# Second cross-attention: the expert-output gathers issued at the first row maximum of a tile instead of behind the row statistics

## The reference, cut to what matters

```python
# x: rows after the second attention; y: expert outputs; gw: the two gate weights of a row
x  = x + gw[:, 0] * y[first expert of the row] + gw[:, 1] * y[second expert of the row]
h  = layernorm(x)                      # rows of the queries, second cross-attention
q  = h @ Wq + bq ;  k = ctx @ Wk + bk ;  v = ctx @ Wv + bv      # 16 heads of 16
p  = softmax(q k^T / 4 + mask)         # 64 queries x 256 keys per sequence and head
x  = x + (p v) @ Wo + bo
```

## Time and profile before

| what | value |
|---|---|
| runs of the kernel before | 1083.7, 1084.77 and 1091.38 us, median 1084.77 us |
| the profiled execution | 1086.17 us, span of its instructions 1084.4 us |
| busy share of the span | TensorE 94%, VectorE 59%, ScalarE 44%, GpSimd 22% |
| second cross-attention | from about 736 to 900 us of the span |
| gathers of this stage | 16, in 8 pairs, 0.94 to 1.04 us each on GpSimd |

### The profile page before, as it was taken

The page is one execution under the profiler, slowest core; times in us unless marked ns, Lnnn a source line. Parts: engine busy times, 40 slices in busy tenths (PEclk is TensorE's granted clock), DMA queues, the critical chain, the costliest instruction groups (busy, mean ns, idle before and its releaser), DMA issues.

```text
span 1084.4 us, 27524 instructions
## 1 busy us (share of the span) xinstructions
PE 1021.5 (94%) x11715; PEld 880.5 (81%) x11715; DVE 639.6 (59%) x1376; ACT 472.6 (44%) x866; POOL 243.7 (22%) x381
## 2 busy tenths in 40 slices
PE   5999999999999899999489999997999998999998
PEld 5888888888887787887389999996888876887887
DVE  5655555455234355775749999976566653454342
ACT  3333333333333656543146677753434333364231
POOL 2311311211211033342403444323211100011000
PEclk9999999999999899998589999999999999999999
DMA  9400000000000800220136567713111002000000
GB/s 298 138 2 21 21 1 21 2 1 1 1 1 10 332 2 3 80 99 12 50 79 233 195 198 273 238 42 88 41 47 35 3 2 68 5 2 2 1 21 19
DMA packets 55672, 72.79 MB, mean 67 GB/s; under 512 B 8504, under 2 KB 48896, under 8 KB 54912
## 3 DMA queue, kind: packets, MB, share of 16 engines
q1 hardware_dynamic: 54016, 66.85, 18.4%
q0 software_dynamic: 1536, 4.20, 1.3%
HBM read 60.02 MB, written 11.01 MB: 66 GB/s over the span
## 4 chain that ended last, share of the span: by engine, by line
PE 83%; DVE 7%; ACT 4%; issue 3%; another core or an unknown queue 1%; POOL 1%; DMA 1%; DVEq 0%; POOLq 0%; ACTq 0%
PE ps L615 8%; PE ps L630 8%; PE ps L2178 7%; PE ps L2194 6%; PE ps L2534 5%; PE ps L1476 4%; PE ps L599 3%; PE ps L647 3%; PE ps L1124 3%; PE ps L1394 3%; PE ps L667 3%; PE ps L1433 2%; PE ps L1493 2%; PE ps L569 2%; PE ps L1049 2%
## 5 line engine op out<-in xcount | busy, mean ns | idle before, releaser
L371 POOL TENSOR_TENSOR rn_tmp<-rn_cur,eps 128x1 f32<-128x1 f32 x48 | 14.6, 304 | 427.1 <-DVE rn_cur L365 427.0
L750 ACT ACTIVATE x0pT<-ps 128x512 f32<-128x512 f32 x64 | 38.4, 600 | 123.5 <-PE ps L630 123.5
L2330 DVE CAST eh_hi<-eh 128x512 fp32r<-128x512 f32 x60 | 69.9, 1165 | 13.7 <-ACT eh L2240 13.7
L2178 PE MATMUL ps<-moe_xT_hi,ew_1hi 128*128 128x256 f32 x240 | 69.7, 290 | 2.3 <-DVE moe_xT_lo L2324 2.3
L2194 PE MATMUL ps<-ew_2hi,eh_hi 128*128 128x256 f32 x240 | 69.4, 289 | 2.4 <-DVE eh_lo L2332 2.4
L2178 PE MATMUL ps<-moe_xT_lo,ew_1hi 128*128 128x256 f32 x240 | 68.8, 287 | 0.0
L2178 PE MATMUL ps<-moe_xT_hi,ew_1lo 128*128 128x256 f32 x240 | 68.7, 286 | 0.0
L2194 PE MATMUL ps<-ew_2hi,eh_lo 128*128 128x256 f32 x240 | 67.0, 279 | 0.0
L2194 PE MATMUL ps<-ew_2lo,eh_hi 128*128 128x256 f32 x240 | 66.9, 279 | 0.0
L2534 PE MATMUL ps<-f,ffw 128*128 128x512 f32 x256 | 60.4, 396 | 0.2 <-DVE f L2507 0.2
L859 DVE TENSOR_TENSOR x0A_lo<-ps,x0A_hi 128x512 fp32r<-128x512 f32 x64 | 41.1, 685 | 31.8 <-ACT x0A_hi L741 31.7
(11 more groups left out here) (330 smaller groups left out, 2827.1 us busy)
## 6 DMA issues: line engine op xcount, KB each, us to landing
ew<-L_ffn_W_dram SPq DMA_DIRECT2D x30, 1024.0 KB, 7.0
x0cin<-ctx_dram SPq DMA_DIRECT2D x8, 512.0 KB, 4.3
x1cin<-ctx_dram SPq DMA_DIRECT2D x8, 512.0 KB, 4.6
xg<-moe_in SPq DMA_DIRECT2D x15, 256.0 KB, 7.6
moe_out<-moe_y SPq DMA_DIRECT2D x15, 256.0 KB, 7.6
moe_in<-padneg SPq DMA_DIRECT2D x3, 1024.0 KB, 12.9
maskrow<-mask_BxS_ik_dram SPq DMA_DIRECT2D x2, 1024.0 KB, 7.5
x0wk<-L_xattn_Wkv_dram SPq DMA_DIRECT2D x1, 1024.0 KB, 9.1
```

The costliest lines, as they stand in the source:

```text
L750: nc.scalar.activation(g.pT[:, u, :], ps[:, S_BANK[u % 2], :], ACT.Exp, scale=64.0 ** -0.5).then_inc(C0.exp, 1)
L2178: last = nc.tensor.matmul(ps[:, n % 3, j * BT:j * BT + BT], w[b % 2][:, i, f * P:f * P + P], v[b % 2][:, i, :], start=(i == 0 and m == 0), ...
L2330: nc.vector.tensor_copy(eh_hi[n % 3][:, :], eh[n % 3][:, :]).then_inc(MO.hi, 1)
```

## The change

GpSimd's order in the second cross-attention is written as a loop over the iterations. The pair of gathers of tile t+2 is now issued in iteration t, behind a wait for `C1.s_ps` at 2t+1, the signal that also starts VectorE's first maximum of tile t. The sets of statistics keep their order, and no other engine's program changes.

```diff
         def pool_x1(pool):
             for t in range(2):
                 moe_collect(pool, t)
-            for phase, t in X1_ROWS:
+            def rstd(phase, t):
                 row_rstd(pool, t, X1_ROWS[phase, t] % 2, phase, X1_ROWS[phase, t])
-                if phase == "x1" and t + 2 < T:
+
+            rstd("x1", 0)
+            rstd("x1", 1)
+            for t in range(T):
+                if t + 2 < T:
+
+                    pool.wait_ge(C1.s_ps, 2 * t + 1)
                     moe_collect(pool, t + 2)
+                if t > 0:
+                    rstd("attn", t - 1)
+                if t + 2 < T:
+                    rstd("x1", t + 2)
+            rstd("attn", T - 1)
```

## The result

The changed kernel takes **1097.34 us** in the median of 17 runs, the kernel before 1084.96 us in 17 runs beside it: ratio **1.0092** [1.0070, 1.0115], 0.9% slower. The forecast was 1080.6 us, and 1097.34 lies outside its range. The ratio leaves out three runs of the changed kernel that count as slow (1102.1 to 1102.6 us; the median of the other 14 is 1095.1), and the profiled execution, which took 1102.3 us, is one of the three.

The account below looks back on a forecast made before the run. TensorE was taken to bound the kernel (83% of the time). Terms -3.93 (tiles 5 to 7), -0.52 (tile 4) and +0.25 (iteration 0) sum to -4.2 us, from the median 1084.77 to 1080.6 us; range 1078 to 1087 us.

Parts of the forecast that it names:

- the 1.31 us: Second cross-attention, iterations 1 to 3: each 1.31 us longer because late gathers hold back TensorE's completion signal to ScalarE.
- the 4.45 of the sum: Gain from removing six pairs from their old places: 3.93 us for tiles 5 to 7, 0.52 for tile 4.
- The recorder's case: Rival: late signals exist only in the profiled execution, or are not the gathers' doing; no effect, 1084.8 us; chance 0.27.
- cost 0: Pairs under the first maximum: a transposes' signal held 0.4 us is covered by VectorE's 0.51 us idle, so 0.
- The half case: Rival: TensorE's own stream is held in `fill_pv`, 0.52 us in five pairs; 1083.2 us; chance 0.11.
- -3.93: Iterations 1 to 3: moving the pairs of tiles 5, 6 and 7 away saves 3 x 1.31 = 3.93 us.
- tile 4's 0.52: Iteration 0: tile 4's pair stretches the last exponent group on TensorE from 0.45 to 0.97 us; removing it saves 0.52.
- Iteration 0: New pair just behind the scores: late transposes' signals delay the next steps by at most 0.5 us; taken as 0.25.
- The data's lateness: Gathered data arrive later before their use in the combine, but still in time: cost 0.
- VectorE's cost: First maximum beside a pair still takes 2.29 us like all others: cost 0.
- GpSimd's wait: GpSimd's added wait for the scores' signal: only roots of statistics over 6 us later stand behind it, cost 0.
- The moved hold: Rival: transposes' signals held 2.14 us at the new place, delaying the second maximum; +2.1 us, 1086.8 us; chance 0.12.

Follow-up runs that it names:

- eight buffers: Kernel before with eight `yg` buffers instead of four, tiles 2 to 7 gathered two at a time behind the first three roots: 1078.62 us on A, 1083.27 us on C.
- the doubled kernel: Changed kernel with each pair of gathers issued twice, the first time into buffers that nobody reads: 1118.76 us on B, ratio 1.0328.

## Why the prediction was wrong

**Where the 1.31 us are, and whose they are: right.** All three recordings of the kernel before have the long beats, and in iterations 1 to 3 alone. Without the late gathers, with plain transfers, or with the pairs elsewhere they are gone, and on B and C the clock-free time falls by 3.7 to 4.7 us, near the 4.45 of the sum (by 0.9 only with eight buffers, which lose in iteration 0 what the loop saves). The plain transfers with the memsets show that it is the indirect transfers.

**The recorder's case: wrong.** Recorded and unrecorded runs agree at equal clock, and on B and C the timed runs of versions without held signals in the loop are faster in clock-free time. The Trainium skill, page "SBUF — State Buffer", section "SBUF: two separate sides", has it that TensorE and ScalarE never wait on anyone; here TensorE was stopped for 0.40 and 0.42 us beside a pair and ran through beside memsets. I did not show whether the memory's ports are what it stands for.

**The step that failed: "cost 0" for the new place.** I looked at which signals fall into the window and found the thin transposes. But a pair beside the dense small matmuls also stops TensorE's own stream: 1.37 us per pair in five iterations, 6.85 us, where I took 0 and named 0.52 as the upper bound. I had taken that bound from the one place where I had seen the stream stretch, the very end of a pair, and had not asked what a whole pair costs under a dense stream. The trace of the kernel before had a row that warned, and I overlooked it, though it stands beside the earlier trace rows: the scatters there start at 499.01 and 500.36, and the 64 matmuls of 18 columns that begin at 500.63 are broken for 0.43 us (the row at 501.81 above) and take 2.79 us, where the 64 that begin at 518.39, 2.0 us behind the start of the next pair, take 2.04 and are not stopped. That is 0.75 us with only the later part of a pair beside the stream; for a whole pair no row bounded the price from above, and the range should have said so. The half case was this mechanism, at less than half its size. With the right size the sum is -3.93 - 0.39 (iteration 0: 17.00 for 17.39, tile 4's 0.52 less 0.13) + 6.85 = +2.5 us.

**The term that was missing: the clock.** +2.5 us would have given 1087.3, slower than before and 0.3 above the upper end of the range. The rest is the granted clock, of which the prediction does not speak. Two falls of 6.83 us followed stopped streams in the first recording, one in the second, five in the doubled kernel, and none between 760 and 899 us in the eleven recordings of kernels that have no pair under `fill_pv` (seven of them not from A). By the mean clocks longer falls came more often too: on B 6 of 11 timed runs of the changed kernel had a mean clock of 0.960 to 0.965, which a fall of 6.83 us alone doesn't give, and the lowest of the 28 runs of the kernel before was 0.970. On B the mean clock of the timed runs went from 0.976 to 0.967. The row that could have warned stands in the windows of before: the clock is at 1.00 over the loop with TensorE busy nearly without a gap, and it had been low in the thin stretch ahead, 0.91 from 740 to 760.

**Iteration 0: right.** I took 0.25; its beat is 17.00 against 16.88 without any pair, so 0.12. **The data's lateness, VectorE's cost, GpSimd's wait:** 0 as predicted, the maximum takes 2.29 us in every row. **The moved hold** did not occur: ScalarE starts the high halves 0.70 us behind the first transpose (837.74 - 837.04), where it is 0.69 with the memsets.

**Open.** What sets the fall near 900 to 914 us, 10 to 20 us long: it comes in some runs of several versions, of the kernel before too on A (6 of 33 at a mean clock of 0.965 or less), and is the larger part of the scatter; whether the changed kernel brings it more often by its earlier falls or by the shift in time, no run tells apart. Why chip A shows no stop, and whether the kernel before has held signals there; there is no recording of it. And what in an indirect transfer it is that TensorE waits for.

## What to carry to other kernels

An indirect transfer issued by GpSimd was not free for TensorE on any chip tried but A: put one pair at a time beside wide matmuls (256 columns here), not beside dense ones of 18 columns or 32 rows, and behind a signal that has been given, not ahead of one that somebody waits for. Before moving something that disturbs a neighbour, ask what it would do to the neighbour's own stream in the new place, search the trace for a like stream beside a like disturbance (here one stood in another stage), and where no row shows it, say that the price is open upwards. Make sure that a chip on which a version shows nothing would have shown the effect at all. And where the engine that bounds is kept at full clock by an unbroken stream, a new gap can have a second price (here in one or two of five iterations, with double pairs in all five): compare the mean granted clock of the runs before explaining a difference of 1% from the order of instructions.

## What the runs showed of the hardware

- A pair of indirect transfers (2.28 us on GpSimd) beside 64 matmuls of 128x18 stops TensorE twice, 0.40 and 0.42 us, beginning some 1.7 us after the pair's start, and costs 1.37 us in all (1.15 on B); two pairs stop it five times. Four gathers in a row opened a gap of 0.60 us even among matmuls of 256 columns, where single pairs opened none.
- Two plain transfers of the same size, or 1.96 us of memsets on GpSimd, stop nothing.
- Stretches at the low clock in this stage and behind it lasted 3.41 to 20.48 us, and differed from run to run of the same kernel.
- Three chips differ in the kernel before by 0.5% in clock-free time (1050.8, 1056.0, 1056.1 us), and a version that gains 0.9% on one is level on another. In the four recordings of the fastest chip, A, no stream is stopped beside an indirect transfer; in the ten others a stream of 64x18 matmuls is, for 0.43 us, at the same place.
